# Sixteen sequences through a macaron block on one core: steps of every queue moved, two of them over a slot's border

## The reference, cut to what matters

```python
x = x + 0.5 * ffn(ln(x))            # 8 experts, 128 -> 512 -> 128, silu, top 2 per token
x = x + mixer(ln(x))                # two mamba blocks and a chunked memory
x = x + 0.5 * ffn(ln(x))            # the same FFN again

def mamba_block(x):                 # d_inner 256, 16 states
    xm, res = split(x @ in_w.T + in_b)
    xm = silu(depthwise_conv4(xm) + conv_b)
    dt, Bm, Cm = split(xm @ xp_w.T)             # 64 + 16 + 16
    delta = softplus(dt @ dt_w.T + dt_b)
    h_t = h_(t-1) * exp(delta_t * A) + (delta_t * u_t) * B_t
    y_t = sum_over_states(h_t * C_t) + xm * D
    return (y * silu(res)) @ out_w.T + out_b

def mixer(x):
    x1 = x + mamba_block(rmsnorm(x))
    return x1 + memory_attend(mamba_block(rmsnorm(x1)))
```

## Time and profile before

| | |
|---|---|
| median of three runs | 1654.6 us (1653.92 to 1655.49) |
| profiled execution, its own time | 1653.32 us, its span 1651.5 us |
| DVE busy | 1391.1 us, 84% |
| PE busy | 1316.8 us, 80% |
| ACT busy | 1251.1 us, 76% |
| POOL busy | 649.9 us, 39% |
| ACT table loads | 182, 233.5 us |

### The profile page before, as it was taken

How to read it: one execution, slowest core, us unless ns; L and a number is a source line. 1 busy time by engine, 2 the same in 40 slices (tenths; PEclk the granted TensorE clock), 3 DMA queues, 4 the chain that set the end, 5 groups by cost and what they waited for, 6 DMA issues and landing times. The chain is left out here.

```text
span 1651.5 us, 29004 instructions
## 1 busy us (share of the span) xinstructions
PE 1316.8 (80%) x8642; PEld 1185.8 (72%) x8642; DVE 1391.1 (84%) x2151; ACT 1251.1 (76%) x2596; POOL 649.9 (39%) x681
## 2 busy tenths in 40 slices
PE   7977568878888688878888688878888787668778
PEld 6967457767778686867777686868877686457668
DVE  3368999989989888989989888989889889988842
ACT  3489658978888787977889787978889688549722
POOL 1212434273625446273624536263534533242220
PEclk9989668989999799999989899997989799779889
DMA  5446347675666667675666667665666665465631
GB/s 189 121 94 139 77 86 158 139 181 133 161 143 145 143 134 179 151 173 119 155 152 139 158 141 182 141 165 117 149 158 142 163 143 106 83 139 117 151 90 45
DMA packets 144230, 227.02 MB, mean 137 GB/s; under 512 B 13648, under 2 KB 79440, under 8 KB 143952
## 3 DMA queue, kind: packets, MB, share of 16 engines
q0 software_dynamic: 39424, 123.76, 38.5%
q1 hardware_dynamic: 104656, 101.41, 21.6%
HBM read 90.90 MB, written 25.17 MB: 70 GB/s over the span
## 5 line engine op out<-in xcount | busy, mean ns | idle before, releaser
L983 ACT ACTIVATE dA<-delta,A 128x255 f32<-128x255 f32 x1024 | 425.7, 495 | 5.3 <-DVE hs L1353 4.4
L1359 DVE TENSOR_TENSOR_SCAN hs<-dA,b_r 128x512 f32<-128x512 f32 x256 | 297.7, 1202 | 13.1 <-PE b_r L671 10.4
L1353 DVE TENSOR_TENSOR_SCAN hs<-dA,dbu 128x1024 f32<-128x1024 f32 x128 | 292.9, 2288 | 16.3 <-ACT dA L983 10.4
L558 PE MATMUL b_out<-w2s,hT 128*128 x1680 | 243.7, 293 | 13.9 <-ACT ys L905 7.8
L1371 DVE TENSOR_TENSOR G<-hs,b_r 128x1024 f32<-128x1024 f32 x192 | 233.4, 1216 | 22.0 <-PE b_r L682 13.9
L544 PE MATMUL b_h<-xsT,wst 128*128 128x128 f32 x1680 | 245.8, 294 | 5.2 <-ACT hT L913 5.2
L558 PEld LDWEIGHTS b_out<-w2s,hT 128*128 128x128 f32 x1680 | 223.1, 206 | 22.0 <-issue 20.9
L854 ACT ACT_TABLE_LOAD x182 | 233.5, 1283 | 3.9 <-PEq L1762 0.7
L544 PEld LDWEIGHTS b_h<-xsT,wst 128*128 128x128 f32 x1680 | 228.5, 210 | 7.5 <-issue 7.0
L671 PE MATMUL b_r<-prm,scaled 128*128 128x128 f32 x1024 | 171.6, 298 | 64.4 <-ACT scaled L999 28.8
L999 ACT ACTIVATE scaled<-duT,dtT 128x256 f32<-128x256 f32 x512 | 217.1, 501 | 0.3
(11 more groups left out here) (181 smaller groups left out, 2220.2 us busy)
## 6 DMA issues: line engine op xcount, KB each, us to landing
wst<-w_dram SPq DMA_DIRECT2D x242, 256.0 KB
acc<-G POOLq DMA_DIRECT2D x96, 512.0 KB
odd<-G POOLq DMA_DIRECT2D x96, 512.0 KB
xsort<-sorted SPq DMA_DIRECT2D x70, 192.0 KB
results<-ys SPq DMA_DIRECT2D x70, 192.0 KB, 3.1
odd<-xd POOLq DMA_DIRECT2D x32, 256.0 KB
xin<-x_dram SPq DMA_DIRECT2D x8, 256.0 KB
sorted<-ys SPq DMA_DIRECT2D x2, 960.0 KB, 7.3
```

What stands on the lines that cost most here:

```text
L558: last = mm(Y[:, i % CH * D:(i % CH + 1) * D], hT[i % NH][:, c, :], w2s[:, e, c, :], start=c == 0, stop=c == HC - 1)
L983: last = do(dA[j % 4][:, d, k, 1:], delta[b][:, k, 1:], ACT.Exp, scale=A[:, k, s:s + 1])
L1353: V.tensor_tensor_scan(flat(hs[j % 2]), flat(dA[j % 4]), flat(dbu[n % 2]), 0.0, ALU.mult, ALU.add)\
L1359: V.tensor_tensor_scan(hs[j % 2][:, d, :, :].rearrange("p h t -> p (h t)"), dA[j % 4][:, d, :, :].rearrange("p h t -> p (h t)"), R[u % 2][ ...
```

## The change

The orders of all four engines are rewritten. There are two new step names. `q` on PE runs pieces of the *next* FFN: `xp` of slot 1 has `q1` (T0) ahead of it, and `k7` and `dx` have `q1` (U0) ahead of them; slot 2 begins its own pieces with T1. `N` on ACT is the leave of that T0, between `xm` and `proj` of slot 1, and `n` is the first decay (`d0`) of the next slot, between `sp` and `dx` of slot 1; slot 2 begins with `d1`. U0's leave stays in slot 2. Beside this, `d7` of slot 1 stands ahead of `r` and `xm`, `k5` ahead of `in`, `D11` behind `out` and `t6`, `t7` ahead of the last two downs; in slot 2 `d2` stands between the leaves of T1 and U1; in slot 3 `fgate` stands ahead of U11, and `t5` behind `turng`; POOL's `fkeep` and accumulates stand elsewhere among scatters and gathers; the other moves are by one place.

```diff
@@ -110,27 +110,36 @@
 
 ORDER = {
     "tensor": (
-        "p1 t0 k0 t1 in t2 p2 k1 t3 p1 t4 p1 k2 xp p1 t5 dt p1 t6 k3 p1 t7 m1 k4 t8 p1 dx p2 m2 k5 t9 p2 t10 m3 t11 k6 p2 m4 k7 p1",
-        "t0 p1 t1 t2 p2 k0 p1 t3 p2 fturn k1 t4 t5 fgate p3 fcount p2 k2 p3 out t6 k3 p5 t7 turn t8 k4 in k5 t9 k6 t10 xp t11 dt k7 dx",
-        "t0 p1 t1 p1 t2 p1 k0 t3 p3 k1 out p1 t4 p1 k2 t5 p1 t6 p1 turn t7 k3 in k4 t8 p1 xp t9 t10 dt k5 p1 t11 p3 k6 p1 dx p2 k7",
-        "t0 t1 p3 t2 k0 p2 t3 p2 fturn p2 fgate k1 p1 t4 fcount t5 p2 turng k2 p1 in k3 t6 p4 k4 t7 t8 xp dt k5 t9 t10 m1 t11 dx k6 m2 m3 k7 m4",
+        "t0 p1 k0 t1 in t2 p2 t3 k1 p1 t4 p2 k2 xp t5 dt p1 t6 k3 p1 t7 m1 k4 t8 p1 dx p2 m2 k5 t9 p2 t10 m3 "
+        "t11 k6 p2 m4 k7 p1",
+        "p1 t0 t1 t2 p1 k0 p1 t3 p3 fturn k1 t4 fgate p2 t5 fcount p3 k2 p2 out t6 p1 k3 p3 t7 p2 k4 t8 turn "
+        "k5 in t9 k6 t10 q1 xp t11 dt q1 k7 dx",
+        "t0 p1 t1 t2 k0 t3 p3 k1 out p1 t4 p1 k2 t5 p1 t6 p1 turn t7 k3 in k4 t8 p1 xp t9 t10 dt k5 p1 t11 p3 "
+        "k6 p1 dx p2 k7",
+        "p1 t0 t1 p2 t2 k0 p3 t3 p1 fturn p1 fgate k1 p1 t4 fcount p3 turng k2 t5 p1 in k3 t6 p4 k4 t7 t8 xp "
+        "dt k5 t9 t10 m1 t11 dx k6 m2 m3 k7 m4",
     ),
     "scalar": (
         "d0 e1 d1 d2 F0 e3 d3 F1 F2 e5 F3 r xm d4 proj d5 sp F4 F5 e7 F6 oT dx F7 d6 d7 v F8 rT",
-        "F9 e1 d0 d1 F10 F11 F12 e3 F13 d2 F14 F15 fxT d3 F16 F17 d4 F18 F19 d5 d6 F20 F21 e5 ftanh F22 F23 e7 F24 turned r xm d7 proj sp dx",
-        "d0 e1 F0 d1 F1 F2 e3 F3 e5 F4 d2 d3 d4 d5 d6 turned d7 e7 F5 F6 r xm F7 proj F8 sp F9 F10 F11 dx",
-        "e1 F12 F13 d0 d1 F14 F15 e3 F16 F17 F18 fxT e5 F19 d2 d3 turned d4 F20 F21 ftanh F22 F23 r xm F24 d5 proj e7 sp d6 oT dx v d7 rT",
+        "F9 e1 d0 d1 F10 F11 F12 e3 F13 d2 F14 F15 fxT d3 F16 F17 d4 F18 F19 d5 d6 F20 F21 F22 e5 ftanh F23 "
+        "e7 F24 turned d7 r xm N proj sp n dx",
+        "d1 e1 F1 F2 e3 d2 F3 e5 F4 d3 d4 d5 d6 turned d7 e7 F5 r xm F6 F7 proj F8 sp F9 F10 F11 dx",
+        "e1 F12 F13 d0 d1 F14 F15 e3 F16 F17 F18 fxT e5 F19 d2 d3 turned d4 F20 F21 ftanh F22 F23 r xm F24 d5 "
+        "proj e7 sp d6 oT dx v d7 rT",
     ),
     "vector": (
-        "b0 s0 g0 s1 gate g1 b2 s2 g2 s3 low b4 g3 delta s4 g4 s5 b6 mask g5 s6 g6 s7 xb g7",
-        "b0 fstats s0 s1 g0 fnorm b2 s2 flog ftop g1 fplace gate g2 s3 b4 xsum g3 un s4 g4 s5 g5 b6 fweights s6 g6 low s7 delta g7 fsum",
-        "b0 s0 s1 g0 gate b2 g1 xsum s2 s3 un g2 b4 lx g3 s4 s5 g4 ln b6 low s6 g5 unx delta g6 s7 g7",
-        "b0 fstats s0 s1 fnorm b2 g0 flog ftop g1 fplace s2 g2 s3 gate g3 b4 s4 fweights g4 s5 low g5 b6 delta s6 mask g6 s7 g7 xb fsum",
+        "b0 s0 g0 s1 gate g1 b2 s2 g2 s3 low b4 g3 delta s4 g4 s5 b6 mask g5 s6 g6 s7 g7 xb",
+        "b0 fstats s0 s1 fnorm g0 b2 s2 flog ftop g1 fplace gate g2 s3 b4 xsum g3 un s4 g4 s5 g5 b6 fweights "
+        "s6 g6 low s7 delta g7 fsum",
+        "b0 s0 s1 g0 gate b2 g1 xsum s2 s3 un g2 b4 g3 lx s4 s5 g4 ln b6 low s6 g5 unx delta g6 s7 g7",
+        "b0 fstats s0 s1 fnorm b2 g0 flog ftop g1 fplace s2 g2 s3 gate g3 b4 s4 fweights g4 s5 low g5 b6 "
+        "delta s6 mask g6 s7 g7 xb fsum",
     ),
     "gpsimd": (
-        "skip a2 a3 a4 a5 a6 a7",
-        "froot skip sc0 sc1 sc2 a2 sc3 sc4 fkeep rms a3 sc5 sc6 sc7 rs a4 ga0 ga1 ga2 ga3 a5 ga4 ga5 ga6 ga7 a6 a7",
-        "skip rms rs a2 a3 lnx rmsx a4 a5 a6 a7",
+        "a2 skip a3 a4 a5 a6 a7",
+        "froot skip sc0 sc1 sc2 sc3 sc4 a2 rms sc5 sc6 sc7 a3 rs a4 ga0 ga1 ga2 ga3 ga4 ga5 ga6 fkeep ga7 a5 "
+        "a6 a7",
+        "rms skip rs a2 a3 lnx rmsx a4 a5 a6 a7",
         "froot skip sc0 sc1 sc2 a2 sc3 sc4 fkeep a3 sc5 sc6 sc7 a4 ga0 ga1 ga2 ga3 a5 ga4 ga5 ga6 ga7 a6 a7",
     ),
 }
@@ -145,6 +154,10 @@
 
 def pieces_in(i):
     return sum(n for name, n in steps("tensor", i) if name == "p")
+
+
+def pieces_ahead(i):
+    return sum(n for name, n in steps("tensor", i) if name == "q")
 
 
 COL, WIDTH = {}, 0
@@ -736,7 +749,8 @@
             def slot(g, i, tail, head, n, nx):
 
 
-                k = pieces_in(i - 1) if i % 2 else 0
+                k = pieces_ahead((i - 2) % 4) + pieces_in(i - 1) if i % 2 else pieces_ahead((i - 1) % 4)
+                early_k = 0
                 for name, num in steps("tensor", i):
                     if name == "t":
                         scan_input(g, i, num)
@@ -747,6 +761,11 @@
                             for x in range(k, k + num):
                                 ffn_piece(n, x)
                         k += num
+                    elif name == "q":
+                        if nx is not None:
+                            for x in range(early_k, early_k + num):
+                                ffn_piece(nx, x)
+                        early_k += num
                     elif name == "fturn":
                         if nx is not None:
                             ffn_turn(nx, (q_duT, 4 * g + i + 1))
@@ -797,6 +816,8 @@
                     elif x == 13:
                         dt_proj(0, 0)
                 du_turn(0, 0)
+                for x in range(pieces_ahead(3)):
+                    ffn_piece(first(1), x)
 
             def finish():
                 tail = (GROUPS - 1, 1)
@@ -1015,6 +1036,9 @@
                 for name, num in steps("scalar", i):
                     if name == "d":
                         decays(g, i, num)
+                    elif name == "n":
+                        if head:
+                            decays(*head, num)
                     elif name == "e":
                         if num == 3 and g == 0 and i == 0:
                             turned_second()
@@ -1022,6 +1046,9 @@
                     elif name == "F":
                         if n is not None:
                             ffn_leave(n, num)
+                    elif name == "N":
+                        if nx is not None:
+                            ffn_leave(nx, num)
                     elif name == "ftanh":
                         if nx is not None:
                             ffn_gate(nx)
@@ -1054,7 +1081,11 @@
                         projections(0, 0)
                     elif x == 14:
                         softplus(0, 0)
+                pass
                 du_turned(0, 0)
+                for name, num in steps("scalar", 3):
+                    if name == "N":
+                        ffn_leave(first(1), num)
 
             def finish():
                 tail = (GROUPS - 1, 1)
```

## The result

The changed kernel takes 1677.2 us (median of 4 runs, 1676.85 to 1677.94) against 1654.9 (1653.92 to 1655.49): a ratio of 1.0136, 95% interval 1.0124 to 1.0148, so 22.4 us slower. The forecast was slower by 11.4 us. The direction and the mechanism were right, the size was half of what was measured; 1677.2 lies just inside the upper end of the range, 1678.

The account below looks back on a forecast made before the run. The prediction took DVE, busy 84% of the span, as the bound. Slot 1's +16.8 and slot 3's -5.4 gave +11.4 us on the profiled 1653.32, 1664.7, or 1666 us with 1.3 for the median; range 1645 to 1678.

Parts of the forecast that it names:

- The read's issue: Slot 1, SP: the read of the sorted rows goes out at 727.1 instead of 725.80, with Y4 1.3 us later.
- The landing: Slot 1: the sorted rows land at 731.3, 4.2 us after the issue; low end 2.1, high end 7.9.
- The chain behind it: Slot 1, T0 to slot 2's first scan: slot 1 +1.7 us with PE at full clock, +3.3 at the lower clock.
- Slot 1 in all: Early T0 and U0 add 2.4 us to each slot 1, seven times, +16.8 us; ends -1.0 and +3.3 each.
- Group 7: Slot 1 of the last group: no last results to wait for, less FFN as cover; taken like the others, +2.4 us.
- k5 and t9: Slot 1: the 1.41 us hole goes, b6 waits 2.6 us for t9; net +1.2, hidden under low's wait, counted 0.
- POOL: Slot 1: reordered POOL steps end the gathers about 1.0 us sooner, a gain covered by the later g7.
- Table loads: ACT, slots 1 and 2: 30 more loads, 38.5 us of ACT, counted 0; up to 2.6 us each without cover.
- Slot 3: fgate ahead of U11 starts 0.9 us sooner in groups 0 to 5, -5.4 us in all; ends 0 and -0.9 each.
- B: Rival: rows land under about 2.5 us after the issue, so the gathers decide slot 1; 1641 us, chance 0.20.
- C: Rival: landing near 730.5 with PE at full clock, slot 1 +0.8 us; 1655 us, chance 0.15.
- D: Rival: ACT becomes the bound as the 30 table loads are not covered, 14 us more; 1680 us, chance 0.08.

Follow-up runs that it names:

- e9: Changed kernel with only POOL's a3 moved back, ahead of sc5 instead of behind sc7: 1674.1 us.
- e3: Changed kernel with all four of POOL's orders as in the kernel before: 1680.8 us.
- e2: Kernel before with only the early T0 and U0, and T0's leave ahead of proj, added: 1678.9 us.
- e4: Changed kernel with SP reading the sorted rows ahead of the first four experts' weights instead of behind them: 1646.7 us.
- e10: Changed kernel with 18 extra matmuls on PE ahead of each early T0, to keep PE busy during the wait: 1678.3 us.
- e7: The kernel of e1 with k5 put behind in_proj again: 1650.5 us.
- e8: The kernel of e1 with ACT's slot 2 grouped as before, d2 beside d3, two table loads fewer per slot 2: 1641.3 us.
- e6: Kernel before with only slot 3's fgate and k1 moved ahead of U11: 1652.2 us.
- e1: Changed kernel with T0 and its leave N moved to the end of slot 1, behind dx, and U0 first in slot 2: 1645.5 us.
- e11: Changed kernel with T0, U0, their leaves and the next slot's d0 back in slot 2, ACT's slot 2 grouped as before: 1640.0 us.

## Why the prediction had the direction right and the size wrong

- *The read's issue.* Replayed to 727.1, which is 36.4 into the slot; measured 36.4. Y4 1.3 us later: 29.0 against 27.6.
- *The landing: the step that failed.* I took 4.2 us from issue to T0; it was 7.5 on average (7.1 to 7.8), so T0 runs at 43.9 and not at 40.6. These 3.3 us in each slot 1 are 20 us over six groups. I reasoned "the same bytes as before", having moved a3 behind the scatters myself in the part on POOL, where I priced it for the gathers alone. a3's place gives 0.8 of the 3.3 (e9) and POOL's whole order 0.9 (e3). 1.7 was there without the rest of the change: e2, with POOL as before, shows 5.9 on average (5.5 to 6.6). The 0.7 between e2 and e3 goes with the other moves and isn't traced further. Only without the weights ahead did the read land about as soon as I took (4.1 to 4.6 in four groups of e4). I had leaned on the lower durations of the earlier trace rows, which are those of stores over the whole run, and the DMA share of 1.0 to 1.2 all through called for the upper half.
- *The chain behind it.* T0 to low is 3.7 us in my sum at full clock, 5.3 with the 1.6 for half clock; measured 5.3 with the clock at 0.50. I took the middle, 0.8 too little. From low to the first scan it was the other way: 9.7 measured, 10.4 in my sum, since `fsum` takes 2.3 us here and 2.8 to 3.3 in the kernel before. There, and in e2, its instructions overlap POOL's product for `skip` (xd<-xm) and get longer. With `skip` behind `rms`, a move that I held at nothing, they don't overlap and `fsum` takes 2.3 to 2.4. The Trainium skill's page TensorE: Matmul & The Clock Gate ("HAM oscillation — how this bites in real kernels"), by which a PE idle on a DMA wait starts its next work cold, was right here: T0 and x_proj ran at 0.50 behind the wait. In e10, where PE did not idle, they ran at 1.00.
- *Slot 1 in all:* +2.4 forecast, +6.1 measured, 22 us too little over six groups. Slot 3 missed the other way by 10 us (below). So half of the error is hidden in the total, by luck.
- *Group 7:* +2.4 forecast, +0.6 in slot 1. Its read went out at 32.9, so T0 found its rows; with T0 early and all else as before (e2) it went out at 35.9 and the slot lost 6.2. DVE's longest wait there, 5.07 us where it had waited 2.01 ahead of g5, comes from the step held at nothing, in_proj behind k5, at half clock; most of it was time that DVE had:

```profile
1498.59 1.22 DVE L1371 TENSOR_TENSOR dbu<-du,b_r 128x1024 f32<-128x1024 f32 x1 [5.07 <-PE b_r L677]
```

- *k5 and t9:* b6 forecast to wait 2.6 us, 2.04 measured, hidden under low's wait, as said. That it may be of use without T0 (e7) I had not seen.
- *POOL:* the gathers' last is issued 0.9 us sooner (45.1 against 46.0 of the slot), as said, and nothing waits for them now; the shorter `fsum` is above.
- *Table loads:* 212 for 182, 30 more, and 0 us in the changed kernel's slot 2 (43.2 and 43.2), right. Without cover I had "up to 2.6 each": e8 gives back 1.7 us per slot 2, of which only 0.5 was a wait for ACT.
- *Slot 3:* -0.9 forecast in groups 0 to 5, -2.6 measured on average in 1 to 6. This is the term that was too small, outside its own ends of 0 and -0.9. I had read the wait for the logits in group 3 only, 1.63 us; in groups 2, 4 and 5 it was 3.0. With fgate and k1 alone (e6) it falls to 0.75 in groups 1 to 4, and the whole gains 1.8 us. In the changed kernel it is 0.3 in groups 1 to 5. Which of the other moves of slots 2 and 3 brings the rest wasn't tried one by one; e1, e8 and e11 all have slot 3 at 49.4 to 50.0, so it doesn't come from the early T0.
- *The rivals.* B (the gathers decide) and C needed a landing under 3.5 us after the issue; in slot 1 the soonest in any run here was 4.1 (e4). D did not occur in the changed kernel; in e1 scans of slot 2 waited for their decays, 0.5 us on average.

## What to carry to other kernels

Before a step that consumes a transfer is moved ahead in an in-order queue, find the transfer's *issue* in the issuing queue and set the landing, not the issue, against the step that will stand behind it; count each queue that holds a consumer, since two of them stood behind these rows. When several moves are made at once, list for each what its DMAs now run beside: the move priced for one reader (a3 for the gathers) made another late. And time the parts apart: here a rest worth -14.5 us was buried under an early T0 that costs 37 beside it. And when a slot gets longer, look at the lengths of its instructions as well as at the waits: more than half of what e1 lost in slot 2 stands in one `un`.

## What the runs showed of the hardware

- The read of 192 KB took 5.5 to 6.6 us from issue to its first use in e2 and 7.1 to 7.8 in the changed kernel, with the DMA engines' share at 1.0 to 1.2; stores of the same size take 3.1 in the median of the whole run before. With the four weight loads behind it in place of ahead (e4) it landed in 4.1 to 4.6 us in four of six groups.
- A PE that waited 7.2 us ran T0 and x_proj at a granted clock of 0.50, x_proj in 3.9 us in place of 2.07. Matmuls of no use in the waiting time kept it at 1.00 and saved 1.5 us per slot 1 where there was a wait, cost 6.5 us where there was none, and left the whole where it was.
- `un`, a TENSOR_SCALAR of DVE that takes 0.27 us alone, took 1.2 to 1.7 us in each of groups 1 to 6 of e1, where it overlapped a TENSOR_TENSOR of POOL (1.02 us), and ended 0.1 us after it; in e8, without the overlap, 0.27. The profile shows no wait there, only the longer instruction.
